# Two graph layers on one core: elu's negative part and the f16 cast of h moved to ScalarE, h recomputed from x1 instead of stored

## The reference

```python
h = maximum(layernorm(x), 0)
wh = h @ W;  wh1 = wh @ a[:128];  wh2 = wh @ a[128:]
e = wh1 + wh2.T;  e = where(e > 0, e, 0.2 * e);  e = where(adj > 0, e, -9e15)
x = x + elu(softmax(e, -1) @ wh)                 # first layer
h = maximum(layernorm(x), 0)
raw = cos_normalize(h @ Wk.T) @ cos_normalize(h @ Wq.T).T
att = softmax(where(adj > 0, raw, -9e15), 1)
prop = att @ h            # rows without any neighbour take h itself
x = x + 0.5 * prop + 0.5 * h                     # second layer
```

## Time and profile before

| what | value |
|---|---|
| time of the runs, median (lowest to highest) | 2169.01 us (2168.13 to 2170.45) |
| the profiled execution's own time | 2168.22 us |
| span of its trace | 2166.4 us |
| mean granted TensorE clock | 0.996 of full speed |
| adj loads, SyncE's queue | 512 of 1024 KB, median 6.2 us from issue to landing |
| h stores, ScalarE's queue | 8 of 512 KB, median 8.3 us |
| h loads, ScalarE's queue | 16 of 256 KB, median 5.9 us |
| x1 loads, ScalarE's queue | 16 of 256 KB, median 5.4 us |

### The profile page before, as it was taken

How to read it: one execution, slowest core, us unless ns; L and a number is a source line. 1 busy time by engine, 2 the same in 40 slices (tenths; PEclk the granted TensorE clock), 3 DMA queues, 4 the chain that set the end, 5 groups by cost and what they waited for, 6 DMA issues and landing times.

```text
span 2166.4 us, 63039 instructions
## 1 busy us (share of the span) xinstructions
PE 2124.2 (98%) x26185; PEld 1721.6 (79%) x26185; DVE 1961.7 (91%) x1679; ACT 1759.5 (81%) x1965; POOL 81.8 (4%) x86
## 2 busy tenths in 40 slices
PE   5999999999999979999999999999999999999998
PEld 5999999999999957777777777777777777777776
DVE  7999999999999878889889889898898898898987
ACT  6987788778787668888888888888888888888886
POOL 1002000000000163000000000000000000000000
PEclk9999999999999999999999999999999999999999
DMA  6899999999999825667676676776676766767663
GB/s 250 341 402 408 401 400 408 398 411 403 404 409 390 332 88 184 222 214 218 200 222 202 207 218 195 222 220 195 214 220 199 222 200 209 220 194 222 214 196 116
DMA packets 120969, 573.58 MB, mean 265 GB/s; under 512 B 9937, under 2 KB 10577, under 8 KB 87633
## 3 DMA queue, kind: packets, MB, share of 16 engines
q1 hardware_dynamic: 109408, 546.02, 72.1%
q10 hardware_dynamic: 11376, 24.91, 3.0%
HBM read 558.24 MB, written 12.65 MB: 264 GB/s over the span
## 4 chain that ended last, share of the span: by engine, by line
PE 93%; DVE 4%; ACT 1%; issue 1%; DMA 1%; POOL 0%; ACTq 0%; DVEq 0%; SPq 0%
PE bank L1302 30%; PE bank L1255 30%; PE bank L1323 21%; PE bank L1318 10%; DVE ring L946 1%; PE bank L1208 1%; DVE hl_buf L764 1%; PE bank L1230 0%; DVE hl_buf L752 0%; DMA ring<-adj 0%; ACT ring L492 0%; ACT hl_buf L569 0%; PE bank L1149 0%; DMA q_buf<-x 0%; DVE q_buf L898 0%
## 5 line engine op out<-in xcount | busy, mean ns | idle before, releaser
L651 ACT ACTIVATE ring<-bank,th_col 128x512 f32<-128x512 f32 x1024 | 648.4, 684 | 231.7 <-PE bank L1302 224.6
L1038 DVE SCALAR_TENSOR_TENSOR ring<-ring 128x2048 f32<-128x2048 int32 x256 | 586.8, 2292 | 148.9 <-ACT ring L651 147.9
L1302 PE MATMUL bank<-v_buf,q_buf 128*128 128x512 f16 x3072 | 706.1, 380 | 3.2 <-ACT ring L651 2.4
L1255 PE MATMUL bank<-v_buf,ring 128*128 128x129 f16 (+1 forms) x12288 | 700.2, 220 | 6.8 <-DVE ring L946 6.7
L1255 PEld LDWEIGHTS bank<-v_buf,ring 128*128 128x128 f16 x12288 | 698.5, 98 | 7.7 <-issue 7.4
L1323 PE MATMUL bank<-u_buf,hl_buf 128*128 (+2 forms) x8192 | 701.6, 220 | 0.0
L1323 PEld LDWEIGHTS bank<-u_buf,hl_buf 128*128 128x128 f16 x8192 | 633.1, 98 | 55.0 <-issue 0.3
L946 DVE SCALAR_TENSOR_TENSOR ring<-r_ring,th_word,ring 128x1024 f32<-128x1024 f32 x512 | 619.8, 1282 | 15.9 <-ACT ring L492 15.9
L1043 DVE TENSOR_TENSOR hl_buf<-ring,hl_buf 128x2048 f16<-128x2048 f32 x256 | 585.0, 2285 | 0.7 <-ACT hl_buf L657 0.7
L1318 PE MATMUL bank<-u_buf,hl_buf 128*128 (+1 forms) x2048 | 559.4, 273 | 0.5 <-DVE hl_buf L1043 0.5
L492 ACT ACTIVATE ring<-ring 128x2048 f32<-128x2048 int32 x256 | 483.2, 1908 | 94.4 <-DMA ring<-adj 90.7
(11 more groups left out here) (146 smaller groups left out, 474.0 us busy)
## 6 DMA issues: line engine op xcount, KB each, us to landing
ring<-adj SPq DMA_DIRECT2D x512, 1024.0 KB, 6.2
r_ring<-a_rows SPq DMA_DIRECT2D x8, 512.0 KB, 7.5
x_dram<-q_buf ACTq DMA_DIRECT2D x8, 512.0 KB, 8.5
h_dram<-hl_buf ACTq DMA_DIRECT2D x8, 512.0 KB, 8.3
r_ring<-x_dram ACTq DMA_DIRECT2D x16, 256.0 KB, 5.4
r_ring<-h_dram ACTq DMA_DIRECT2D x16, 256.0 KB, 5.9
...
```

The source lines that it names most:

```text
L651: ins = nc.scalar.activation(p_ring[:, k, (2 * hf + m) * IW:(2 * hf + m + 1) * IW], bank[:, 2 * hf + m, :], ACT.Exp, scale=q_scale[:, j:j ...
L1038: V.scalar_tensor_tensor(p_ring[:, k, :], adj_ring[:, k, :], 0.0, p_ring[:, k, :], ALU.is_gt, ALU.mult).then_inc(s_m, 1)
L1255: ins = mm(acc0(par, it), weights0(k, ps)[:, it // 4, jj, f], v2[:, bass.ds((2 * j + us) * HALF, D + 1)], start=False, stop=False, skip_gr ...
L1302: ins = mm(bank[:, 2 * hf + m, :], q_buf[:, qs, bass.ds(j * P, P)], k_buf[:, ks, bass.ds(i * IW, IW)], start=(x == 0), stop=(x == 2))
```

## The change

Four things are changed.

1. `negative` is gone from VectorE. `exponential` on ScalarE now first makes Relu(-z) into `e_buf`, waits for itself (`s_neg`), and takes Exp with scale -1. It waits for `s_free`, which `quotient` on the same engine has raised, and no longer for VectorE.
2. The f16 cast of h is made on ScalarE at the end of `normalised` (`s_uh`); VectorE's `split` keeps only the subtraction.
3. h isn't written to DRAM, and the waits for that store are gone.
4. In the second layer only x1 is loaded. ScalarE makes h of it in a new part `h_again(i)`, four Relu instructions at unit (3, 1) of each chunk, (3, 3) in the first; VectorE's `kept` waits for it. For that `rstd` and `nbias` keep a column for every tile.

```diff
-EPI0 = ("den", "neg", "elu", "x1", "stats") + LN + ("hi", "lo")
+EPI0 = ("den", "elu", "x1", "stats") + LN + ("lo",)
...
                 def exponential():
-                    act.wait_ge(s_ev, at("neg"))
-                    nc.scalar.activation(e_buf, e_buf, ACT.Exp).then_inc(s_ea, 1)
+                    act.wait_ge(s_free, c + 1)
+                    nc.scalar.activation(e_buf, z_buf, ACT.Relu, scale=-1.0).then_inc(s_neg, 1)
+                    act.wait_ge(s_neg, c + 1)
+                    nc.scalar.activation(e_buf, e_buf, ACT.Exp, scale=-1.0).then_inc(s_ea, 1)
...
                     if lo == 0:
                         act.wait_ge(s_ev, at("nbias"))
-                        if not (isinstance(c, int) and c == 0):
-                            act.wait_ge(s_hw, 16 * c)
...
                     act.wait_ge(s_ea, 3 * c + 3)
-                    act.dma_start(h_dram[:, bass.ds(c * C0, C0)], h_buf).then_inc(s_hw, 16)
+                    nc.scalar.activation(u_tiles[:, bass.ds(c * IT0, IT0), UH:UH + D],
+                                         h_buf.rearrange("p (t f) -> p t f", f=D), ACT.Copy).then_inc(s_uh, 1)
...
-            act.wait_ge(s_hw, 16 * NC0)
...
-                act.dma_start(e_h, h_dram[:, bass.ds(i * IW, IW)]).then_inc(s_fin, 16)
+
+            def h_again(i):
+                act.wait_ge(s_fin, 16 * (i + 1))
+                for it in range(IT1):
+                    t = i * IT1 + it
+                    ins = nc.scalar.activation(e_h[:, it * P:(it + 1) * P], e_x1[:, it * P:(it + 1) * P], ACT.Relu,
+                                               bias=nbias[:, t:t + 1], scale=rstd[:, t:t + 1])
+                ins.then_inc(s_hr, 1)
...
-                             (2, 3): lambda: load_factors(i + 2)}
+                             (2, 3): lambda: load_factors(i + 2), (3, 1): lambda: h_again(i)}
...
-                             (3, 1): lambda: load_factors(2), (3, 2): lambda: residual(0)}
+                             (3, 1): lambda: load_factors(2), (3, 2): lambda: residual(0), (3, 3): lambda: h_again(0)}
...
-                def negative():
-                    dve.wait_ge(s_free, c + 1)
-                    V.tensor_scalar(e_buf, z_buf, 0.0, None, ALU.min).then_inc(s_ev, 1)
...
                 def split():
-                    dve.wait_ge(s_ea, 3 * c + 3)
+                    dve.wait_ge(s_uh, c + 1)
                     h8 = h_buf.rearrange("p (t f) -> p t f", f=D)
                     hi = u_tiles[:, bass.ds(c * IT0, IT0), UH:UH + D]
-                    V.tensor_copy(hi, h8).then_inc(s_ev, 1)
-                    dve.wait_ge(s_ev, at("hi"))
                     V.tensor_tensor(u_tiles[:, bass.ds(c * IT0, IT0), HALF:US], h8, hi, ALU.subtract).then_inc(s_ev, 1)
...
-                    parts = dict(zip((3, 7, 10, 11, 15, 19), epilogue(c - 1, 1 - par)))
+                    parts = dict(zip((3, 10, 11, 15, 19), epilogue(c - 1, 1 - par)))
...
             copy_ht(7)
-            negative()
             copy_ht(8)
...
-                    dve.wait_ge(s_fin, 32 * (i + 1))
+                    dve.wait_ge(s_hr, i + 1)
```

More of the change, by code:

```diff
@@ L84, in graph_layers @@
         x1_dram = nc.dram_tensor("x1_dram", [P, N], F32, kind="Internal").ap()
-        h_dram = nc.dram_tensor("h_dram", [P, N], F32, kind="Internal").ap()
         k_rows = nc.dram_tensor("k_rows", [T, P], F32, kind="Internal").ap()
@@ L569, in normalised @@
                         ins = nc.scalar.activation(h_buf[:, it * P:(it + 1) * P], xs[:, bass.ds(c * C0 + it * P, P)],
-                                                   ACT.Relu, bias=nbias[:, it:it + 1], scale=rstd[:, it:it + 1])
+                                                   ACT.Relu, bias=nbias[:, c * IT0 + it:c * IT0 + it + 1],
+                                                   scale=rstd[:, c * IT0 + it:c * IT0 + it + 1])
                     if hi < IT0:
@@ L737, in variance, with scale_bias @@
                 V.scalar_tensor_tensor(var, sq, 1.0 / D, var, ALU.mult, ALU.add).then_inc(done, 1)
-            def scale_bias(lo, hi, at, done):
-                V.reciprocal(rstd[:, lo:hi], small[:, 4, lo:hi]).then_inc(done, 1)
+            def scale_bias(lo, hi, at, done, first=0):
+                tiles = slice(first + lo, first + hi)
+                V.reciprocal(rstd[:, tiles], small[:, 4, lo:hi]).then_inc(done, 1)
                 dve.wait_ge(done, at("rstd"))
-                V.scalar_tensor_tensor(nbias[:, lo:hi], small[:, 1, lo:hi], -0.5, rstd[:, lo:hi],
+                V.scalar_tensor_tensor(nbias[:, tiles], small[:, 1, lo:hi], -0.5, rstd[:, tiles],
                                        ALU.mult, ALU.mult).then_inc(done, 1)
@@ L879, in scales @@
                     dve.wait_ge(s_ea, 3 * c + 2)
-                    scale_bias(0, IT0, at, s_ev)
+                    scale_bias(0, IT0, at, s_ev, c * IT0)
                 def split():
-                    dve.wait_ge(s_ea, 3 * c + 3)
+                    dve.wait_ge(s_uh, c + 1)
                     h8 = h_buf.rearrange("p (t f) -> p t f", f=D)
                     hi = u_tiles[:, bass.ds(c * IT0, IT0), UH:UH + D]
-                    V.tensor_copy(hi, h8).then_inc(s_ev, 1)
-                    dve.wait_ge(s_ev, at("hi"))
                     V.tensor_tensor(u_tiles[:, bass.ds(c * IT0, IT0), HALF:US], h8, hi, ALU.subtract).then_inc(s_ev, 1)
-                return denominators, negative, residual, moments, scales, split
+                return denominators, residual, moments, scales, split
             def copy_ht(g):
@@ L992, in key_low @@
                                 ALU.subtract).then_inc(s_lo, 1)
-            denominators, negative, residual, moments, scales, split = epilogue(NC0 - 1, 1)
+            denominators, residual, moments, scales, split = epilogue(NC0 - 1, 1)
             copy_ht(2)
```

4 lines of the change are left out of this document (3 added, 1 removed).

## The result

The changed kernel takes 2174.87 us, median of 11 runs (2171.86 to 2178.53); before takes 2169.12 us (11 runs, 2166.36 to 2171.10). The ratio is 1.0025, 95% interval 1.0018 to 1.0033: 5.4 us slower (3.9 to 7.2). Forecast were 2174.5 us and slower. The profiled execution took 2171.86 us, the shortest of its eleven, with a span of 2170.0 us; before 2168.22 and 2166.4.

What follows compares the result with a forecast made beforehand. TensorE was taken as the bound by a hair, VectorE 97% busy in the first layer. 2168.2 profiled + 4.5 first layer + 1.0 transition = 2173.7, with 0.8 for the median 2174.5 us; 8-in-10 range 2169.5 to 2178.

Steps and rivals of the forecast that it cites:

- Relu ahead of Exp: First layer, ScalarE behind unit 9: the added Relu delays unit 10 by 1.0 us, bounds 0 and 1.1.
- `negative` off VectorE: First layer, behind unit 7: the 0.69 us saved gives nothing back, as VectorE then waits longer at unit 10.
- Cast, 0.6 later at unit 18: End of `normalised`: the cast replaces the store's issue on ScalarE, so unit 18's Sign and VectorE come 0.6 us later.
- split, 0.7 saved: VectorE between units 19 and 20: without the cast the step falls from 1.79 to 1.1 us.
- Loss 2.16 - d in each chunk: Chunks 2 to 7; d is VectorE's lead over TensorE at unit 12 before; losses sum to 5.94 us, 4.5 net.
- Transition, 1.0: Between the layers: Relu 0.3 and cast 0.7 make the first scores 1.0 us later, between 0.7 and 1.8.
- h store, counted nothing: First layer: 512 KB less stored per chunk lets loads land sooner, but VectorE waits for none there; counted 0.
- Second layer, 0: `h_again`'s four instructions, 1.6 us, 16 times, are covered by ScalarE's idle time; removing the h loads gives nothing.
- hidden: Rival: unit 9's load lands sooner, the Relu fills ScalarE's wait; 2168.5 us, half hidden 2171.5; chance 0.27.
- VectorE was the bound: Rival: each microsecond off VectorE comes off the time, 9.7 us in 7 chunks, 2159; a gain had chance 0.04.
- no refund: Rival: `split` gains nothing or the cast costs more; needed lead 1.9 for 1.16, loss grows 4.4 us, 2179; chance 0.12.
- second layer exposed: Rival: the second layer pays for `h_again`, 16 x 1.6 = 26 us, 2195 to 2200; chance 0.02.

Runs made afterwards that it cites:

- e5: Changed kernel with the Relu moved to behind unit 7 on ScalarE and the cast back on VectorE; ratio to before 0.9988.
- e3: Before with h neither stored nor loaded but made again in the second layer, `negative` and cast staying on VectorE; ratio to before 0.9985.
- e1: Before with only `negative` moved to ScalarE, as a Relu ahead of Exp; ratio to before 1.0018.
- e7: Before with h made again in the second layer, h still stored by ScalarE but read by nobody; ratio to before 1.0003.
- e2: Before with only the f16 cast of h moved to ScalarE, behind the issue of the h store; ratio to before 1.0011.
- e10: Changed kernel with h still stored by ScalarE ahead of its cast, read by nobody; ratio to before 1.0033.
- e8: Changed kernel with the Relu behind unit 7 and the cast behind unit 18's Sign on ScalarE; ratio to before 0.9988.
- e9: Before with h made again and still stored, GpSimd in place of ScalarE issuing the first seven stores; ratio to before 0.9991.
- e11: Changed kernel with Relu behind unit 7, cast behind unit 18's Sign, and the last chunk's cast on VectorE; ratio to before 0.9985.
- e4: Changed kernel with only the Relu moved, to behind unit 7 on ScalarE in place of unit 9; ratio to before 1.0001.
- e6: Before with `negative` moved to ScalarE as a Relu ahead of Exp, and that Relu made twice; ratio to before 1.0060.

## Why the prediction was right, point by point

- *Relu ahead of Exp, 1.0 later at unit 10.* Right: 5.14 in place of 4.20, 0.94. VectorE's waits there are 1.64 to 2.49 us in chunks 3 to 7, as the 1.5 to 2.5 forecast; chunk 2 has 0.87.
- *`negative` off VectorE is worth nothing.* Right. e5 against e3 is the clean test: 0.69 us per chunk less on an engine at 97%, 4.8 us in sum, and no gain (e5 is the slower by 0.0003). The rule of the Trainium skill weighed in the forecast (Perfetto Trace Analysis, Optimizing Scalar/DVE Operations), that a move to ScalarE may pay when VectorE is saturated, didn't hold here: VectorE's busy time fell by 9.4 us and the kernel got 5.4 slower.
- *Cast, 0.6 later at unit 18; split, 0.7 saved.* Right: 0.48 to 0.54 later (1.49 against 1.01, 1.00 against 0.46), and 0.74 saved.
- *Loss 2.16 - d in each chunk.* Forecast 1.26, 0.20, 1.14, 1.00, 1.66, 0.68; measured 1.08, 0.19, 0.59, 1.06, 0.96, 0.81. The form of the rule is right. With d read in every trace as the prediction reads it, and the loss of chunks 2 to 6 in the same way as above, loss + d is nearly the same number for one order of instructions wherever a chunk loses: 1.25 to 1.27 in before, `e1` and `e7`; 1.41 to 1.44 in `e2` and `e10`, which have issue and cast ahead of unit 18; 0.62 to 0.70 (once 0.81) in `e3`, `e5`, `e8`, `e9` and `e11`, which have neither; 1.02 to 1.04 in the changed kernel and `e4`, where the forecast had 1.16. (Chunk 7 needs 0.2 less. The exceptions are chunks 2 and 5 of `e6`, 2.56 and 2.34 in place of 1.26: the stretches at half the clock, and the 2.4 us named above.) The term: 3.2 measured, 4.5 forecast. Of the 1.3 missing, 0.8 is the lead needed, 0.2 chunk 7 and the rest d. The values of d are another matter: they sum to 7.0 us in before and to 3.2 in `e7`, with the same instructions (`e7` has d -0.17, 0.89, 0.88, -0.46, 0.74 and 1.28 and loses 1.43, 0.37, 0.39, 1.72, 0.52 and 0; the changed kernel has d -0.04, 0.84, 0.43, -0.02, 0.06 and 0.00). That they sum to 1.3 in the changed kernel, near the 1.0 forecast, and the likeness chunk by chunk, is partly luck.
- *Unit 29 of chunk 7.* Missed: 1.25 us. The prediction let chunk 7 come off with its own stall and never asked who else waits for a VectorE without lead. It fills the gap of the term above, so the first layer came to 4.5 by two errors that cancel.
- *Transition, 1.0.* Right: 0.8. The Relu's share was put at 0.3 and is 0.1 (e1 has 0.1 too, with two Relu it is 1.2: one of them just fits under VectorE's copy); the cast's share of 0.7 is 0.7.
- *h store, counted nothing.* This is the weak step. Its issue slot was counted, in the cast's 0.6, but not that the cast only uses up a gain that was there to be had: alone, leaving out the store gives 3.3 us (e3). The parts measured apart, +3.9, +2.4 and -3.3, make +3.0, the whole +5.4. Whether they fail to add isn't shown: each part is uncertain by some 2 us, and in the first scores the parts make +8.2 us where the whole has +5.0, the other way round.
- *Second layer, 0.* Right. ScalarE's four new Relu at unit 30 shift one Exp:

```profile
954.65 1.64 ACT L688 ACTIVATE r_ring<-r_ring,nbias,rstd 128x128 f32<-128x128 f32 x4
956.19 2.40 ACT L653 ACTIVATE ring<-bank,th_col 128x512 f32<-128x512 f32 x4
...
960.95 2.56 ACT L653 ACTIVATE ring<-bank,th_col 128x512 f32<-128x512 f32 x4 [0.56 <-PE bank L1305]
```

  The Exp behind them starts with no idle time, the next one already waits 0.56 us for TensorE again. Equal length behind the first scores was forecast; it is 1.5 shorter, by the clock.
- *Sum.* 2173.7 for the profiled execution, measured 2171.9; 1.5 of the 1.8 is that clock. Then 0.8 was added for the median, and this execution turned out 3.0 below its own. The 0.4 us between forecast and median are better than the reasoning deserves; the ratio says 5.4 +- 1.6 for a forecast of 5.5. Some of the 5.4 may be the clock: the mean granted clock is 0.9947 over the eleven executions of the changed kernel and 0.9953 over 33 of before, and within the changed kernel's own a straight line through their times falls by 1.5 us for each 0.001 of it (2178.4 and 2178.5 us at 0.993; 2171.9, 2173.9 and 2171.9 at 0.996). That makes an estimate of 1 us, for which the forecast had no term.

Of the rivals, *hidden* and *VectorE was the bound* fall with e4 and e5; *no refund* falls with `split`, 1.05 us; *second layer exposed* falls with e3.
